# Scores' minimum with a per-row scale in one DVE operation, and squares, sums, masks and first turns moved

## The chip, the cores and the metric

The kernel runs on one core of one Trainium2 chip. The metric is the device time of one execution in microseconds (us). Its engines are named as the profile names them: PE (matrix products), PEld (its weight loads), DVE (vector), ACT (activation), POOL (GpSimd) and SP, whose queue issues every DMA of this kernel. Each engine works through its own list of instructions in order; semaphores tie the lists together.

## What is computed

Two layers on x (2 x 512 x 1024) and a context of 2 x 1024 x 1024. What matters here:

```
x = x + fake_quant(LN(x)) @ fake_quant(ctx)                         # L0 product
x = x + LN(x) @ W.T + b + low-rank experts mixed by a router        # ffn
x = x + attention(LN(x), ctx, ctx, mask)     # 32 query heads, 8 key/value heads, d = 128, rotary
x = x + LN(x) @ W_up.T + low-rank expert of the top gate
softmax:  P = exp(raw/sqrt(d) + mask - rowmax),  out = P V / sum(P),  then out @ wo
```

Products that need more than 16 bits are made of three matmuls, on high and low halves: low by high, high by low, high by high (`mm3`, lines 43 to 45). In attention the halves are float16. Scales that are powers of two, taken from sums of squares of wk, the context, wq and wo, keep the float16 halves in range.

## The kernel before, in words

**Keys and values (to about 435 us).** `steps()` runs 64 steps `s`: a group of four (0 to 3, and 32 to 35 for the second batch), then one at a time. A step multiplies one half of one slice of wv or wk by the transposed context of its batch (24 matmuls), the result ends in one of five PSUM banks, and `kv_end` on DVE, POOL and ACT scales, rotates and splits it before SP stores it. Tables name the step at which side work is done: `SQUARE_STEPS` (squares of wq on ACT, 64 of the 128 tiles; `square`, line 1971, one pass over 128x512 with a sum per row) and `SQUARE_LOAD_STEP` (their loads on SP, seven buffers), `KEY_SUM_AT` (a tiny product on PE that sums squares of one wk slice over the partitions, `key_squares`, line 873, then `key_scale` on DVE), `X_QUANTISE_AT`, `C_QUANTISE_AT`, `SUM_AT` (`sum_product`, line 899, ahead of the step's own products) and `L0_AT` (the L0 product, line 912). At the start ACT splits w0, c0, c1, w1, c2 to c7 into halves (`split_hi`, line 1892) and squares c0 to c7 and w1 (`key_square`, line 1980); on DVE `context_squares` (line 1301) adds the eight sums after splitting w2; PE's `key_squares(0)` needs both. Key sum 5 is at step 20.

**ffn (to about 550 us).** PE turns and multiplies tiles f0 to f7 and turns h0 to h7; ACT takes the roots and high halves, and in between the squares 64 to 127 of wq and wo. SP loads those, stores tiles, and from `load_h` on loads what attention needs.

**Attention (about 550 to 1950 us).** 64 heads H (32 per batch), four row tiles of 128 each, n = 4H + i in all. In every slot (p, w) PE does a quarter of the query product of head p + 2 (`q_part`), a quarter of the output product (`wo_part`), one tile of scores (`scores(4p + w + 3)`, into one of two PSUM pairs) and once per head the values product (`values(p - 1)`). One tile n passes: PE scores; DVE `scores_max` (line 1728: scores + mask written to `psb`, the row maximum accumulated into column i of `c`; then line 1731, a 128x1 multiply by the scale and by -1; its wait on the semaphore of the maximum stands between the two); ACT `exp` (line 2139, scale and bias per row, sum accumulated); DVE `row_scale` (lines 1739 and 1741); ACT `p_hi` (line 2146); DVE `p_lo` (line 1746); SP `turn_p` (line 689, a DMA transpose). ACT's `p_hi(n)` waits for the transpose of n - 3 to land, PE's `scores(n)` for the maximum of n - 2. At the end of a slot group w = 3 DVE rotates the queries (`q_end`), POOL adds and splits them (`q_lo`, lines 2306, 2308), ACT copies the high half (`q_hi`) and then the output's (`o_hi`), DVE its low half (`o_lo`, line 1751), for which `wo_part` waits every second head. POOL also scales and splits the weights of wq and wo that SP streams in (lines 2296, 2302), and SP's loads wait for POOL's earlier splits.

**Entry of attention.** DVE: `q_end(0)`, `scale_mask` of tile 0 (line 1718), `q_end(1)`, mask 1, `scores_max(0)`, `h_lo(7)` (for which PE's `q_part(2, 0)` waits), and so on; `q_end(2)` after slot (0, 0); in slot (0, 1) `output_sums` and `output_scales` (lines 1568 to 1581, twelve operations of at most 16 numbers per row), for which PE has added up the squares of wo and of the value scales (`square_sums("v")`, in slot (0, 1), in bank 7). SP: masks 2 and 3 are issued after `store_h(7)`, which waits for `h_lo(7)`; ahead of `turn_p(1)` stand four weight loads, of which wo (2, 1) waits for POOL's split of wq 6 and wq 9 for that of wq 7.

Of the kernel before, what the change touches and what calls it, by code (L numbers as in the profile page):

```python
# [112 lines left out]
SQUARE_STEPS = sorted([*range(6, 28), *range(38, 60), *range(40, 60)])  # L113
# [8 lines left out]
def build_in(nc, ctx, A, out):  # L122
# [276 lines left out]
    KEY_SUM_AT = {0: 0, 5: 1, 9: 2, 13: 3, 17: 4, 20: 5, 25: 6, 29: 7, 32: "c1"}  # L399
# [48 lines left out]
    v_ws = signal("v_ws", [("w", j) for j in range(11)] + [("v", j) for j in range(12)])  # L448
# [6 lines left out]
    v_nmax = signal("v_nmax", range(256))  # L455
# [99 lines left out]
    def sync_program(e):  # L555
# [163 lines left out]
        for n in range(71, 105):  # L719
            load_square(n)  # L720
        for i in range(4):
            store_h(i)
            for n in (range(105, 110), range(110, 116), range(116, 120), range(120, 125))[i]:
                load_square(n)
# [10 lines left out]
        for n in range(125, 128):  # L735
            load_square(n)
# [21 lines left out]
        load_mask(0, 1)  # L758
        load_w(("q", 6))
        load_v(0)  # L760
# [3 lines left out]
        for i in range(2, 4):  # L764
            load_mask(0, i)
# [4 lines left out]
        for p in range(66):  # L770
# [62 lines left out]
    def tensor_program(e):  # L833
# [89 lines left out]
        def square_sums(what):  # L923
# [6 lines left out]
            else:  # L930
                e.wait_ge(a_sq.sem, a_sq[127])
                e.wait_ge(v_ws.sem, v_ws["v", 1])
                e.wait_ge(v_qr.sem, v_qr[0])
                e.matmul(ps[:, 7, 0:64], twos[:, :], squares[:, 64:128], start=True, stop=True)
                e.matmul(ps[:, 7, 64:80], twos[:, :], sc[:, 32:48], start=True, stop=True).then_inc(t_rt.sem, 1)
# [160 lines left out]
        def scores(n):  # L1096
# [6 lines left out]
            if n < 2:  # L1103
                e.wait_ge(v_x2.sem, v_x2[7 - n, 1])
            else:
# [104 lines left out]
        for w in range(4):  # L1210
            q_part(0, w, 7)
        e.wait_ge(v_rt.sem, v_rt[1, 3])
# [8 lines left out]
        for p in range(66):  # L1221
            for w in range(4):
                if (p, w) == (0, 1):
                    square_sums("v")
# [50 lines left out]
    def vector_program(e):  # L1275
# [272 lines left out]
        def query_scale():  # L1548
# [10 lines left out]
            e.reciprocal(kst[:, 38:40], sc[:, 22:24]).then_inc(v_ws.sem, 1)  # L1559

# [5 lines left out]
        def output_sums():  # L1566
            e.wait_ge(t_rt.sem, t_rt["v"])
            e.tensor_reduce(sc[:, 0:1], ps[:, 7, 0:64], AX, ALU.add).then_inc(v_ws.sem, 1)
            e.tensor_reduce(sc[:, 1:3], ps[:, 7, 64:80].rearrange("p (a b) -> p a b", a=2), AX, ALU.add).then_inc(v_ws.sem, 1)
# [846 lines left out]
```

## Time and profile before

| | |
|---|---|
| three runs | 2071.3, 2071.78 (median), 2072.1 us |
| the profiled execution | 2071.39 us |
| its span, first to last instruction | 2069.6 us |
| mean granted TensorE clock over the span | 0.989 |
| instructions | 26390 |
| scores' maxima (line 1728), exponentials (line 2139) | 256 each |

The profiled execution lies 0.4 us below the median. A row of the timeline gives start and duration in us, then engine, line, operation, written tile <- read tiles, and in brackets how long the engine had been idle and what ended that. PE's records overlap: at full clock one matmul of 512 columns follows another every 0.22 us, though each is written as 0.38.

### The profile page before, as it was taken

The numbers are of one execution on the slowest core, as the hardware profiler recorded it, in microseconds if no ns is written. First come the engines' busy times: TensorE is split into PE (matmuls) and PEld (weight loads), VectorE is DVE, ScalarE is ACT, GpSimd is POOL, SyncE is SP. The second block draws the span as 40 slices with busy tenths as digits, with TensorE's granted clock in tenths as the row PEclk, the third lists the DMA queues.
The fourth block names the chain that finished last, engine by engine and source line by source line (L and its number), as shares of the span: only waits on it lengthen the run. The fifth ranks groups of instructions, "written<-read, shape, count | busy, mean of one in ns | idle before, by whom it ended". The sixth has DMA issues, their size and how long they took to land.

```text
span 2069.6 us, 26390 instructions
## 1 busy us (share of the span) xinstructions
PE 1987.7 (96%) x9136; PEld 1113.4 (54%) x9140; DVE 1639.9 (79%) x2960; ACT 1128.5 (55%) x1722; POOL 1234.6 (60%) x751
## 2 busy tenths in 40 slices
PE   7999999999979999999999999999999999999899
PEld 6877786878634444444444444444444444444487
DVE  5777786576788888888888888888898898888743
ACT  5453553345556666665666665556665666656410
POOL 1542352422158777777777777777777877775500
PEclk9999999999989999999999999999999999999999
DMA  7652575445988787887778798977777787877611
GB/s 247 207 175 89 181 233 165 144 147 189 302 197 166 149 173 146 179 162 157 160 147 174 163 218 198 200 172 163 164 161 158 159 176 147 166 154 149 187 65 69
DMA packets 673382, 349.56 MB, mean 169 GB/s; under 512 B 576769, under 2 KB 601601, under 8 KB 673249
## 3 DMA queue, kind: packets, MB, share of 16 engines
q1 hardware_dynamic: 673248, 347.87, 70.0%
q8 instruction: 73, 1.20, 0.2%
q14 instruction: 61, 0.49, 0.1%
HBM read 173.73 MB, written 31.46 MB: 99 GB/s over the span
## 4 chain that ended last, share of the span: by engine, by line
PE 75%; DVE 8%; issue 3%; DMA 2%; ACT 2%; POOL 1%; SPq 0%; ACTq 0%; DVEq 0%; POOLq 0%
PE ps L43 25%; PE ps L44 24%; PE ps L45 24%; PE ps L912 1%; DMA pT<-pp 1%; POOL u_sb L2253 1%; DVE psb L1728 1%; DVE pp L1746 1%; DVE t_sb L1290 1%; DVE t_sb L1292 1%; DVE u_sb L1289 0%; DVE vhl_sb L1386 0%; PE ps L919 0%; DMA raw<-in_ctx 0%; ACT wh L1892 0%
## 5 line engine op out<-in xcount | busy, mean ns | idle before, releaser
L1746 DVE SCALAR_TENSOR_TENSOR pp<-psb,st,pp 128x1024 f16<-128x1024 f32 x256 | 423.0, 1652 | 3.4 <-ACT pp L2146 1.3
L2139 ACT ACTIVATE psb<-psb,st,sc 128x1024 f32<-128x1024 f32 x256 | 317.6, 1240 | 174.3 <-DVE st L1731 174.3
L2146 ACT ACTIVATE pp<-psb,st 128x1024 f16<-128x1024 f32 x256 | 293.4, 1146 | 165.0 <-DVE st L1741 158.5
L1728 DVE CUSTOM_DVE_ANT_0 psb<-ps,mask 128x1024 f32<-128x1024 f32 x256 | 311.8, 1218 | 32.5 <-PE ps L45 31.2
L2296 POOL TENSOR_SCALAR araw<-araw,kst 128x512 f32<-128x512 f32 x128 | 283.0, 2211 | 49.4 <-DMA araw<-in_wq 49.4
L2296 POOL TENSOR_SCALAR araw<-araw,sc 128x512 f32<-128x512 f32 x128 | 258.3, 2018 | 0.0
L2302 POOL TENSOR_TENSOR wol<-araw,woh 128x512 f16<-128x512 f32 x128 | 149.5, 1168 | 137.5 <-ACT woh L2072 137.5
L43 PE MATMUL ps<-woh,osb 128*128 128x512 f16 x512 | 195.0, 381 | 23.8 <-issue 19.0
L1762 DVE SCALAR_TENSOR_TENSOR x_lo<-ps,sc,x_lo 128x512 f32<-128x512 f32 x256 | 190.4, 744 | 20.4 <-PE ps L45 20.4
L43 PE MATMUL ps<-ksb,qsb 128*128 128x512 f16 x512 | 195.3, 381 | 9.5 <-DVE st L1728 8.1
L43 PE MATMUL ps<-pT,vsb 128*128 128x512 f16 x512 | 194.4, 380 | 6.0 <-DMA pT<-pp 5.2
L44 PE MATMUL ps<-ksb,qsb 128*128 128x512 f16 x512 | 195.3, 381 | 0.0
L45 PE MATMUL ps<-ksb,qsb 128*128 128x512 f16 x512 | 195.1, 381 | 0.0
L44 PE MATMUL ps<-wol,osb 128*128 128x512 f16 x512 | 194.9, 381 | 0.0
L45 PE MATMUL ps<-woh,osb 128*128 128x512 f16 x512 | 194.8, 380 | 0.0
L44 PE MATMUL ps<-pT,vsb 128*128 128x512 f16 x512 | 194.7, 380 | 0.0
L45 PE MATMUL ps<-pT,vsb 128*128 128x512 f16 x512 | 194.6, 380 | 0.0
L43 PE MATMUL ps<-slots,wl 128*128 128x512 f32 x448 | 180.7, 403 | 12.5 <-ACT slots L1892 9.6
L2306 POOL TENSOR_TENSOR ua<-ua,ta 128x512 f32<-128x512 f32 x64 | 137.4, 2146 | 82.9 <-DVE ta L1277 82.9
L2302 POOL TENSOR_TENSOR wql<-araw,wqh 128x512 f16<-128x512 f32 x128 | 149.8, 1171 | 59.5 <-ACT wqh L2072 59.5
L44 PE MATMUL ps<-slots,wh 128*128 128x512 f32 x448 | 177.2, 396 | 0.0
L45 PE MATMUL ps<-slots,wh 128*128 128x512 f32 x448 | 177.0, 395 | 0.0
(303 smaller groups left out, 3946.4 us busy)
## 6 DMA issues: line engine op xcount, KB each, us to landing
araw<-in_wq SPq DMA_DIRECT2D x128, 256.0 KB, 4.5
araw<-in_wo SPq DMA_DIRECT2D x128, 256.0 KB, 4.3
scan<-in_wq SPq DMA_DIRECT2D x64, 256.0 KB, 4.5
scan<-in_wo SPq DMA_DIRECT2D x64, 256.0 KB, 4.9
raw<-in_wv SPq DMA_DIRECT2D x16, 512.0 KB, 4.6
raw<-in_ctxT SPq DMA_DIRECT2D x16, 512.0 KB, 4.0
raw<-in_wk SPq DMA_DIRECT2D x16, 512.0 KB, 5.7
raw<-in_ctx SPq DMA_DIRECT2D x16, 512.0 KB, 4.6
```

Of the source, the lines that this page charges most:

```text
L43: e.matmul(dst, ll, rh, start=start, stop=False)
L44: e.matmul(dst, lh, rl, start=False, stop=False)
L45: return e.matmul(dst, lh, rh, start=False, stop=stop)
L912: m = e.matmul(bank(L0_BANKS[n % 3]), a1T[:, k, i * 128:i * 128 + 128], bq[:, k, nh * 512:nh * 512 + 512], start=k == 0, stop=k == 7)
L1728: e.tensor_tensor_reduce(out=psb[:, n % 3, :], in0=pair(n % 2 * 2), in1=mask[:, i, :], scale=1.0, scalar=LOWEST, op0=ALU.add, op1=ALU.max, ...
L1746: e.scalar_tensor_tensor(out=pp[:, r, 1024:2048], in0=psb[:, r, :], scalar=st[:, n // 4 % 4, 16 + i:17 + i], in1=pp[:, r, 0:1024], op0=ALU ...
L1762: e.scalar_tensor_tensor(out=xs, in0=bank(6 + i % 2), scalar=sc[:, 30 + (q - 2) // 32:31 + (q - 2) // 32], in1=xs, op0=ALU.mult, op1=ALU.a ...
L2139: e.activation(P, P, ACT.Exp, bias=c[:, 4 + i:5 + i], scale=sc[:, 23 - H // 32:24 - H // 32], accum_out=c[:, 8 + i:9 + i]).then_inc(a_exp. ...
L2146: e.activation(pp[:, r, 0:1024], psb[:, r, :], ACT.Copy, scale=st[:, n // 4 % 4, 16 + i:17 + i]).then_inc(a_ph.sem, 1)
L2296: e.tensor_scalar(w_raw(n), w_raw(n), scale, None, ALU.mult).then_inc(p_ws.sem, 1)
L2302: e.tensor_tensor(w_dst(key, 1), w_raw(n), w_dst(key, 0), ALU.subtract).then_inc(p_wlo.sem, 1)
L2306: e.tensor_tensor(ua[:, :], ua[:, :], ta[:, :], ALU.add).then_inc(p_qu.sem, 1)
```

## The change

In `scores_max` the one DVE operation now adds the mask, multiplies by `sc[:, 23 - H//32]`, a value per row that `query_scale` has turned negative with one more small operation, and accumulates the minimum; line 1731 and its semaphore are gone, and `exp` takes the minimum as its bias and -1 as its scale. The rest moves: squares between steps, key sum 5 from step 20 to 21, the start's key squares between the splits, the squares of the ffn stage each a little earlier (none after h5's root), their loads with them; `square_sums("v")` to just after `q_part(0, ...)`, in bank 3, and `output_sums` and `output_scales` to just after `q_end(0)`, ahead of the first mask; `q_end(2)` from slot (0, 0) to (0, 1); on SP masks 2 and 3 ahead of the first values' load and of `store_h(7)`, load wo (2, 1) behind `turn_p(1)` and load wq 9 behind `turn_p(2)`. `SQUARE_STEPS` had one square at steps 6 to 27, 38 and 39 and two at 40 to 59; now one at 8 to 17, 25, 26 and 38, and three at 19, 20, 21, 23, 24 and 48 to 59.

```diff
-SQUARE_STEPS = sorted([*range(6, 28), *range(38, 60), *range(40, 60)])
+SQUARE_STEPS = sorted([*range(8, 18), 38] + [19, 20, 21, 23, 24] * 3 + [25, 26] + [*range(48, 60)] * 3)
-    KEY_SUM_AT = {0: 0, 5: 1, 9: 2, 13: 3, 17: 4, 20: 5, 25: 6, 29: 7, 32: "c1"}
+    KEY_SUM_AT = {0: 0, 5: 1, 9: 2, 13: 3, 17: 4, 21: 5, 25: 6, 29: 7, 32: "c1"}
...
         load_mask(0, 1)
+        load_mask(0, 2)
         load_w(("q", 6))
+        load_mask(0, 3)
         load_v(0)
         store_x2(7)
         store_h(7)
         load_w(("q", 7))
-        for i in range(2, 4):
-            load_mask(0, i)
...
             if p < 64:
                 load_w(("o", p + 2, 0))
+            if 0 < p < 64:
                 load_w(("o", p + 2, 1))
-            if 2 * p + 9 < 128:
-                load_w(("q", 2 * p + 9))
+                if 2 * p + 9 < 128:
+                    load_w(("q", 2 * p + 9))
...
                     turn_p(4 * p + w + 1)
+                if (p, w) == (0, 0):
+                    load_w(("o", 2, 1))
+                if (p, w) == (0, 1):
+                    load_w(("q", 9))
...
             q_part(0, w, 7)
+        square_sums("v")
         e.wait_ge(v_rt.sem, v_rt[1, 3])
...
+            e.wait_ge(v_ws.sem, v_ws["w", 10])
+            e.tensor_scalar(sc[:, 22:24], sc[:, 22:24], -1.0, None, ALU.mult).then_inc(v_ws.sem, 1)
...
-            e.tensor_tensor_reduce(out=psb[:, n % 3, :], in0=pair(n % 2 * 2), in1=mask[:, i, :], scale=1.0, scalar=LOWEST,
-                                   op0=ALU.add, op1=ALU.max, accum_out=c[:, i:i + 1]).then_inc(v_max.sem, 1)
-            e.wait_ge(v_max.sem, v_max[n])
-            e.tensor_scalar(c[:, 4 + i:5 + i], c[:, i:i + 1], sc[:, 23 - H // 32:24 - H // 32], -1.0, ALU.mult,
-                            ALU.mult).then_inc(v_nmax.sem, 1)
+            e.tensor_tensor_reduce(out=psb[:, n % 3, :], in0=pair(n % 2 * 2), in1=mask[:, i, :], scale=sc[:, 23 - H // 32:24 - H // 32],
+                                   scalar=-LOWEST, op0=ALU.add, op1=ALU.min, accum_out=c[:, i:i + 1]).then_inc(v_max.sem, 1)
...
         q_end(0, 7)
+        output_sums()
+        output_scales()
         scale_mask(0, 0)
...
-                if (p, w) == (0, 0):
+                if (p, w) == (0, 1):
                     q_end(2)
-                if (p, w) == (0, 1):
-                    output_sums()
-                    output_scales()
...
         for key in SPLIT_ORDER[:10]:
             split_hi(key)
-            if key in ("c5", "c6", "c7"):
-                key_square(("c", int(key[1:]) - 5))
-        for c in range(3, 8):
-            key_square(("c", c))
+            for done in {"c2": [0], "c3": [1], "c4": [2], "c5": [3, 4], "c6": [5], "c7": [6, 7]}.get(key, []):
+                key_square(("c", done))
         key_square(0)
...
-            e.wait_ge(v_nmax.sem, v_nmax[n])
-            e.activation(P, P, ACT.Exp, bias=c[:, 4 + i:5 + i], scale=sc[:, 23 - H // 32:24 - H // 32], accum_out=c[:, 8 + i:9 + i]).then_inc(a_exp.sem, 1)
+            e.wait_ge(v_max.sem, v_max[n])
+            e.activation(P, P, ACT.Exp, bias=c[:, i:i + 1], scale=-1.0, accum_out=c[:, 8 + i:9 + i]).then_inc(a_exp.sem, 1)
```

## Rows read from the trace of the kernel before

**Rows 1.** The page: busy time, share of the span and instructions of each engine

```profile
PE 1987.7 (96%) x9136; PEld 1113.4 (54%) x9140; DVE 1639.9 (79%) x2960; ACT 1128.5 (55%) x1722; POOL 1234.6 (60%) x751
```

**Rows 2.** Windows: busy us (x instructions) per engine, PEclk, DMA share, GB/s

```profile
36.10:39.50 3.40, 3.40 (x9) 2.61 (x9) 3.07 (x14) 2.57 (x5) 0.00 (x0) 0.50 0.07 22
135.10:141.90 6.80, 5.83 (x15) 4.53 (x16) 4.50 (x10) 3.81 (x9) 2.45 (x2) 0.50 0.54 155
322.90:326.30 3.40, 3.40 (x10) 2.67 (x9) 2.22 (x7) 2.23 (x7) 2.20 (x1) 0.51 1.03 266
589.10:592.50 3.40, 3.25 (x8) 1.16 (x9) 3.19 (x10) 2.14 (x5) 2.38 (x2) 0.51 0.11 22
595.90:602.70 6.80, 6.04 (x15) 2.20 (x16) 5.66 (x13) 5.01 (x7) 0.73 (x1) 0.50 1.10 201
900.00:1100.00 200.00, 196.46 (x904) 87.28 (x903) 171.76 (x302) 123.14 (x170) 153.77 (x94) 1.00 0.78 162
```

**Rows 3.** Waits of PE, whole span: us in total, times, longest us

```profile
PE ps L43 <- DVE st L1728: 8.1, 4, 3.5
...
PE ps L873 <- ACT junk L1980: 3.1, 1, 3.1
...
PE ps L899 <- POOL ctab L2265: 3.0, 1, 3.0
...
PE ps L873 <- DVE ksq L1301: 2.4, 1, 2.4
```

**Rows 4.** Waits of PE from 620 to 1895 us

```profile
PE ps L43 <- issue: 17.3, 24, 1.7
```

**Rows 5.** Timeline (start us, us) around the end of the first step

```profile
30.82 1.06 ACT L1980 ACTIVATE junk<-slots 128x1024 bf16<-128x1024 f32 x1
...
35.40 0.15 DVE L1301 TENSOR_REDUCE ksq<-ksq 128x1 f32<-128x8 f32 x1
```

**Rows 6.** Timeline at step 20 of the key and value stage

```profile
134.78 1.06 ACT L1980 ACTIVATE junk<-wh 128x1024 bf16<-128x1024 f32 x1
```

**Rows 7.** Timeline at steps 47 to 50

```profile
311.63 0.62 ACT L1971 ACTIVATE scan<-scan 128x512 f32<-128x512 f32 x1
...
320.45 2.13 POOL L2265 TENSOR_TENSOR ctab<-ctab,bq 128x1024 f16<-128x1024 f16 x1
```

**Rows 8.** Timeline at the entry of attention

```profile
564.01 1.06 DVE L1718 TENSOR_SCALAR mask<-mask,kst 128x1024 f32<-128x1024 f32 x1 [0.83 <-DMA mask<-in_mask]
...
566.51 0.69 DVE L1277 TENSOR_TENSOR ua<-ps,cosq 128x512 f32<-128x512 f32 x1 [1.44 <-POOL qsb L2308]
...
572.35 0.59 PE L43 MATMUL ps<-hTa,wql 128*128 128x512 f16 x1 [3.12 <-DVE hst L1277]
...
578.35 0.93 DVE L1718 TENSOR_SCALAR mask<-mask,kst 128x1024 f32<-128x1024 f32 x1 [2.23 <-DMA mask<-in_mask]
...
589.36 0.21 DVE L1568 TENSOR_REDUCE sc<-ps 128x1 f32<-128x64 f32 x1
...
589.89 1.12 DVE L1297 TENSOR_SCALAR sc<-sc 128x3 int32<-128x3 int32 x1
...
591.38 3.00 SPq L689 DMA_TRANSPOSE pT<-pp  x1
...
592.75 0.36 DVE L1581 TENSOR_SCALAR vso<-vsc,sc 128x8 f32<-128x8 f32 x2
```

**Rows 9.** Timeline in the middle of attention

```profile
993.43 1.16 POOL L2302 TENSOR_TENSOR wol<-araw,woh 128x512 f16<-128x512 f32 x1 [0.60 <-ACT woh L2072]
993.49 0.21 DVE L1731 TENSOR_SCALAR st<-st,sc 128x1 f32<-128x1 f32 x1
...
993.62 2.05 DVE L1746 SCALAR_TENSOR_TENSOR pp<-psb,st,pp 128x1024 f16<-128x1024 f32 x1
...
995.77 0.15 DVE L1741 TENSOR_SCALAR st<-st 128x1 f32<-128x1 f32 x1
...
1004.54 0.38 PE L43 MATMUL ps<-woh,osb 128*128 128x512 f16 x1 [0.69 <-issue]
```

More of the change, by code:

```diff
@@ L447, in build_in @@
     v_h2 = signal("v_h2", range(8))
-    v_ws = signal("v_ws", [("w", j) for j in range(11)] + [("v", j) for j in range(12)])
+    v_ws = signal("v_ws", [("w", j) for j in range(12)] + [("v", j) for j in range(12)])
     v_rt = signal("v_rt", [(b, j) for b in range(2) for j in range(8)])
@@ L718, in sync_program @@
             load_w(("q", n))
-        for n in range(71, 105):
+        for n in range(71, 113):
             load_square(n)
@@ L722, in sync_program @@
             store_h(i)
-            for n in (range(105, 110), range(110, 116), range(116, 120), range(120, 125))[i]:
+            for n in (range(113, 119), range(119, 124), range(124, 128), [])[i]:
                 load_square(n)
@@ L932, in square_sums @@
                 e.wait_ge(v_ws.sem, v_ws["v", 1])
-                e.wait_ge(v_qr.sem, v_qr[0])
-                e.matmul(ps[:, 7, 0:64], twos[:, :], squares[:, 64:128], start=True, stop=True)
-                e.matmul(ps[:, 7, 64:80], twos[:, :], sc[:, 32:48], start=True, stop=True).then_inc(t_rt.sem, 1)
+                e.wait_ge(v_x2.sem, v_x2[6, 1])
+                e.matmul(ps[:, 3, 0:64], twos[:, :], squares[:, 64:128], start=True, stop=True)
+                e.matmul(ps[:, 3, 64:80], twos[:, :], sc[:, 32:48], start=True, stop=True).then_inc(t_rt.sem, 1)
         def ffn_turn(tile):
@@ L2074, in scalar_program @@
         ffn_hi(4)
-        for n in range(72, 75):
+        for n in range(72, 77):
             square(n)
         root(("f", 6))
-        for n in range(75, 76):
+        for n in range(77, 80):
             square(n)
         ffn_hi(5)
-        for n in range(76, 84):
+        for n in range(80, 89):
             square(n)
@@ L2085, in scalar_program @@
         ffn_hi(6)
-        for n in range(84, 90):
+        for n in range(89, 97):
             square(n)
@@ L2090, in scalar_program @@
         ffn_hi(7)
-        for n in range(90, 98):
+        for n in range(97, 106):
             square(n)
@@ L2096, in scalar_program @@
         router_exp(1)
-        for n in range(98, 101):
+        for n in range(106, 109):
             square(n)
         lora_hi(1)
-        for n in range(101, 103):
+        for n in range(109, 112):
             square(n)
@@ L2103, in scalar_program @@
         h_hi(1)
-        for n in range(103, 109):
+        for n in range(112, 118):
             square(n)
@@ L2107, in scalar_program @@
         h_hi(2)
-        for n in range(109, 113):
+        for n in range(118, 123):
             square(n)
@@ L2111, in scalar_program @@
         h_hi(3)
-        for n in range(113, 118):
+        for n in range(123, 128):
             square(n)
@@ L2115, in scalar_program @@
         h_hi(4)
-        for n in range(118, 121):
-            square(n)
         root(("h", 6))
         h_hi(5)
-        for n in range(121, 125):
-            square(n)
         root(("h", 7))
         h_hi(6)
-        for n in range(125, 128):
-            square(n)
         split_w(("q", 3))
```

11 lines of the change are left out of this document (4 added, 7 removed).

## The prediction

> **What bounds the kernel now.** I read the page first. PE is busy 96% of the span [rows 1], so only what makes PE wait, or run slow, can be gained or lost. The windows then show short stretches in which PE ran at half the granted clock, 1.2 GHz, ten in the span; five stand in [rows 2], each right behind one of PE's waits. PE's waits by releaser name the events: at the start for the key squares' sum (2.4), at step 20 for a key square on ACT (3.1), at step 50 for a sum on POOL (3.0), at the entry of attention for DVE's maxima [rows 3], and in the body of attention 24 waits, 17.3 us together [rows 4]. The timelines around these [rows 5 to 9] say what is late at each. A matmul that is not held follows the last one after 0.22 us whatever DVE does: DVE is busy 171.8 of 200 us in mid-attention, PE 196.5 [rows 2]. DVE time saved is therefore worth nothing by itself; it pays only in front of one of these waits.
>
> **The sum, part by part.** It is made against the profiled execution, 2071.39 us, which lies 0.4 below the median; I forecast the same quantity for the median. A measurement of this kernel tells about 0.2%, 4.1 us, from no change.
>
> *Start.* ACT does six key squares in a row behind c7, 1.24 apart, the last of them at 30.8, then w1's, and only then w2; DVE adds the sums behind w2's low half, at 35.40 [rows 5], and PE waits 2.4. Spread over the gaps between the arriving tiles, the squares end some 3 us sooner, by my replay at 28.5, w2 is split while PE still works on the first group, and the sum is ready at about 32.9, when PE ends it. Gone: 2.4 of wait and half of 3.4 us at half clock, 1.7 [rows 2, 3]; together 4.1. The later splits c3 to c7 come up to 2 us later, but PE reaches c7 only 1.3 or more behind it. DVE's and SP's work moves forward by 2.5 only, so a load of weights may be short: I take 3.4, bounds 1 and 4.1.
>
> *Key sum 5 from step 20 to 21.* PE waits 3.1 for the key square that starts at 134.78 [rows 3, 6], and loses half of 5.8 busy us at half clock, 2.9 [rows 2]. A step later PE has 5.2 us of products in front of the sum. The squares that now crowd steps 19 to 21 stand behind the key square on ACT. What is late next is `a_turn(3)` behind step 22, which needs DVE's `key_scale(5)`; it has a step of time. I take 5.8, bounds 3 and 6.
>
> *Step 50.* PE waits 3.0 for POOL's last sum, 320.45 to 322.6, then loses 1.7 to the clock [rows 2, 3, 7]. That sum hangs on the split of w25 on ACT, which stood behind two squares of 0.62 each [rows 7], and this on an identical pair before w23. All four are gone from the steps 39 to 47: 2.5 off the chain, which leaves 0.5 of wait; I take the low stretch to go with the rest. Of 3.0 + 1.7 that is 4.2 less what rounding of my replay may hide, 4.0; bounds 0 (another wait takes the place) and 4.7. The square dropped at step 27 gives 0.5 at the second batch's start.
>
> *What is added.* Three squares a step from 48 on, and one or two more ahead of the roots of f6 and h2: at each of three places 0.62 or twice that falls on ACT ahead of something PE waits for. The others lie beside ACT's idle time; were that gone, each would cost its 0.62. The small operation behind `query_scale` is one more of 0.2 there. Together 1.5, bounds 0 and 3. DMA bytes are the same; SP's loads of squares come nearer to their use, in steps where ACT has nothing else to do.
>
> *Entry of attention.* Output sums and scales took DVE from 589.36 to 593.1, 3.75 us, of which one operation on three numbers took 1.12 [rows 8]. Now they stand ahead of the first mask, where DVE was idle 0.83 for its DMA and 1.44 for POOL: 2.3 cover, so mask 0, `q_end(1)` and `h_lo(7)` come 1.5 later, and PE's wait of 3.1 at 572.35 [rows 8] grows to 4.6. If nothing blocks the twelve operations (2.0 us) that is 0; if POOL holds each of the last four, 3.7. `square_sums("v")`, 0.6 of PE, moves to where PE stood 0.8 for POOL; it costs nothing. In return, masks 2 and 3 leave the queue that stood behind `h_lo(7)`, and the idle 2.23 before mask 2 [rows 8] goes; the 3.75 leave the chain between the fifth and sixth maximum; and `turn_p(1)`, which left SP's queue at 591.38 [rows 8] although its tile was ready at 582.8, goes out at about 583, so ACT's `p_hi(4)` no longer waits for it. PE spends here 7.4 of the 8.1 us of waits for maxima [rows 3] and half of 3.25 and 6.04 busy us at low clock [rows 2], 12.0 in all. It will not all go: DVE needs 3.0 per tile where PE, with only scores to do, needs 1.3. My replay leaves waits of 1.7, 2.3 and 1.9 before the sixth and seventh scores and the second values product. 12.0 - 1.5 - 5.9 = 4.6; I take 4.2, bounds -2 and 10.
>
> *One operation fewer per tile, 256 times.* From the start of line 1731 to the next start are 0.13 us [rows 9]. The scale as a per-row operand is not in the trace for this operation; line 1731, with one such operand, takes 0.21 and line 1741, with constants alone, 0.15 [rows 9], so I add 0.06 (bounds -0.1 and 1.2, a second pass). Net about 0.1 per tile. But the tile loop does not run on DVE: line 1746 starts at 993.62, POOL's split at 993.43, and 1746 then takes 2.05 where alone it takes 1.28 [rows 9], so it ends 1.07 behind POOL's end. An earlier start waits longer for POOL. Only the last maximum before `q_end` is not behind such a wait. POOL, ACT and `o_lo` then carry that 0.1 to `wo_part`, whose wait (0.69 at 1004.54) is one of the 24. 24 x 0.12 = 2.9, bounds -3 and 17.3.
>
> The Trainium skill (SBUF — State Buffer, Who interferes with whom) has a rule for this: a vector operation with two SBUF inputs, or a two-port one, and a GpSimd one exclude each other, and whoever issues first keeps the shared port to its end. The 2.05 and the 1.12 agree. Without the rule, all three maxima between two syncs would count, 24 x 0.3 = 7.2 in place of 2.9.
>
> *The change of batch and the end.* Exponentials start 0.2 sooner and DVE leads for some four tiles at each: 1.4, bounds 0 and 4.
>
> Sum: 3.4 + 5.8 + 0.5 + 4.0 - 1.5 + 4.2 + 2.9 + 1.4 = 20.7. 2071.4 - 20.7 = 2050.7; I say **2051**, this case's own range 2044 to 2058.
>
> **Rivals.** (A) *The forecast*, 0.57.
>
> (B) *The order on the port turns over.* Line 1746 starts 0.19 behind POOL at 993.43; one operation less is 0.13 of that. Where DVE comes first, it ends 0.8 to 0.9 sooner, `q_end` follows, and all 24 waits vanish: 17.3 in place of 2.9, 2036.5. For it: the margin is 0.06 to 0.1, and eight of 32 head pairs show no such wait even now. Against it: the row operand's 0.06 eats half. 0.15. The skill's rule on the port, by which the first to issue keeps it, is what this would be.
>
> (C) *Early gains are taken back by queues.* The operations ahead of the first mask are each held by POOL (3.7 instead of 1.5, and a second stretch at low clock), so that the entry of attention gives nothing, and at step 50 the context tile's load or the extra DMA is late in place of ACT: 20.7 - 4.2 - 4.0 - 2 = 10.5, 2061. For it: 1.12 and 2.23 [rows 8] show both kinds. 0.20.
>
> (D) *Slower: the minimum with a row scale is not the same pass.* Place: line 1728. DVE has 28 us idle in 200 at mid-attention [rows 2], 0.7 per tile. If the scaled form made two passes, 2.4 instead of 1.2, it would add 1.1 per tile net: (1.1 - 0.7) x 256 = 102, less 17 of the other gains, 2156. It decides from about 1.6 us per operation: each 0.1 above 1.3 costs up to 24 x 0.3 = 7 us at the `wo_part` waits. For: no row shows the form. Against: the add and the maximum already share one pass, and row scales cost 0.06 elsewhere. 0.04.
>
> (E) *Within 0.2%*: (C) with the start's gain lost too to a late weight load and new low-clock stretches. 2068. 0.04.
>
> **Numbers.** Faster: A, B, C, 0.92; same 0.04; slower 0.04. The range 2040 to 2062 leaves out most of B (0.11), D and E: 0.19.
>
> **What would show it.** Right: PE has no wait at the key sums of the first group and step 21, and no half clock there; the sum on POOL at step 50 costs PE under 1 us; line 1728 takes 1.26 to 1.30; line 1731 is gone; the sums and scales stand before the first mask and `h_lo(7)` is 1 to 2 us later relative to `q_end(0)`; `turn_p(1)` goes out within 1 us of its tile; waits of PE for DVE's maxima at the entry fall from 7.4 to about 4; some 24 waits of 0.6 remain before `wo_part`. Wrong: these waits gone (B); a wait over 5 us for `h_lo(7)`, or still 3 at step 50 (C); line 1728 above 1.6 (D); new low-clock stretches between 40 and 130 or 320 and 440.

## The result and the profile after

| | before | changed |
|---|---|---|
| median (runs) | 2071.94 us (4) | 2034.64 us (4) |
| profiled span | 2069.6 us | 2034.3 us |
| ratio, 95% interval | | 0.9819, 0.9802 to 0.9836 |

The change gains 37.3 us, 1.8%. I had forecast 20.7, in a range of 2040 to 2062: the sign was right, the size was not. Run again beside other kernels, the changed kernel gave 0.9835 (0.982 to 0.985); the kernel before had medians of 2069.2 to 2075.6 from one set of runs to the next, so everything below is told as a ratio to its own runs of before, or from one trace. One execution of one variant (`loads_back`) took 4170.5 us, twice the time of its other three, and is in no ratio.

To place the gain I count PE's matmuls. The n-th matmul is the same work in both kernels, so the time between two of them is the length of a stage. Up to four records are missing in a trace (two near 167 us, two near 349), about 1 us. Stages are named by the time they have in the kernel before.

| stage | before | changed, two traces | gained | forecast |
|---|---|---|---|---|
| to 240 us (start, step 20, second batch) | 240.2 | 235.4, 233.7 | 4.8, 6.5 | 9.7 |
| 240 to 540 (step 50, feed-forward) | 299.9 | 299.4, 297.3 | 0.5, 2.6 | 2.5 |
| 540 to 640 (entry of attention) | 100.0 | 92.0, 90.7 | 8.0, 9.3 | 4.2 |
| 640 to 1895 (body of attention) | 1254.9 | 1233.3, 1235.6 | 21.6, 19.3 | 4.3 |
| the rest | 169.8 | 170.4, 169.7 | -0.6, 0.1 | 0 |

The miss is the body. The first line of the page, the windows (columns as in [rows 2]) and PE's waits of the changed kernel:

```profile
PE 1976.0 (97%) x9140; PEld 1114.2 (55%) x9140; DVE 1605.2 (79%) x2705; ACT 1105.9 (54%) x1722; POOL 1247.3 (61%) x751
```

```profile
156.80:160.20 3.40, 3.40 (x9) 1.25 (x10) 3.36 (x4) 3.34 (x12) 0.89 (x1) 0.51 0.24 83
...
566.40:569.80 3.40, 3.40 (x9) 1.14 (x8) 2.89 (x6) 2.82 (x6) 3.26 (x3) 0.51 0.65 207
586.80:590.20 3.40, 3.40 (x11) 1.14 (x9) 3.30 (x9) 2.58 (x5) 0.01 (x1) 0.52 1.03 190
900.00:1100.00 200.00, 199.15 (x921) 89.56 (x920) 167.59 (x267) 122.83 (x174) 159.99 (x97) 1.00 0.80 166
```

Waits of PE in the whole span:

```profile
PE ps L43 <- DVE st L1733: 5.3, 3, 3.1
...
PE ps L914 <- DVE tmp L1437: 4.0, 1, 4.0
...
PE ps L901 <- POOL ctab L2258: 2.2, 1, 2.2
```

and from 620 to 1895 us, against [rows 4]:

```profile
PE ps L43 <- issue: 5.7, 25, 1.4
```

In 200 us of mid-attention PE now does 921 matmuls where it did 904 [rows 2]. The wait ahead of the output product is still there, about as often as before, but it is 0.2 us and no longer 0.7. The half-clock stretches at 36, 135 and 323 us are gone, a new one stands at 156.8 behind a new wait of 4.0 for the first layer's terms, and of the two at the entry that are shown in [rows 2] the long one at 595.9 is gone. Others move from trace to trace: one at 518.7 is in this trace and not in the second one of the changed kernel; the one at the change of batch, at 1299.0 before, is missing here and stands at 1269.6 in the second.

Where in the body PE gets its 21.6 us back can be read from its starts. They follow each other after 0.22, and I add up by how much a start comes later than that, where it is over 0.02:

| us over the pitch, in the body | output product | values product | the rest |
|---|---|---|---|
| before | 21.2 in 24 | 11.8 in 58 | 1.9 |
| changed, two traces | 8.2 in 24, 8.7 in 22 | 4.4 in 5, 5.2 in 7 | 0.7, 1.7 |

So 13.0 come at the output product, 0.54 at each of its 24 late starts, and 7.4 at the values product. Most of the late starts there are of 0.1 to 0.2 us, too short for the list of waits. One of them before, and the same place in the changed kernel, in the timeline of PE:

```profile
995.49 0.38 PE L45 MATMUL ps<-ksb,qsb 128*128 128x512 f16 x1
995.92 0.38 PE L43 MATMUL ps<-pT,vsb 128*128 128x512 f16 x1
```

```profile
977.65 0.38 PE L45 MATMUL ps<-ksb,qsb 128*128 128x512 f16 x1
977.86 0.38 PE L43 MATMUL ps<-pT,vsb 128*128 128x512 f16 x1
```

The first pair is 0.43 apart, the second 0.21.

### The profile page after: what moved, and what is told of

Same layout as the page of the kernel before. It is cut to its first block, busy times and chain, and to the rows that moved or that the text cites. A ratio compares the mean times of both kernels' runs of the same rounds, so it can differ in the third digit from the quotient of the medians.

```text
span 2034.3 us, 26140 instructions
## 1 busy us (share of the span) xinstructions
PE 1976.0 (97%) x9140; PEld 1114.2 (55%) x9140; DVE 1605.2 (79%) x2705; ACT 1105.9 (54%) x1722; POOL 1247.3 (61%) x751
## 4 chain that ended last, share of the span: by engine, by line
PE 78%; DVE 7%; issue 2%; DMA 2%; ACT 1%; POOL 1%; SPq 1%; ACTq 0%; DVEq 0%; POOLq 0%
PE ps L43 25%; PE ps L44 25%; PE ps L45 25%; PE ps L914 1%; DMA pT<-pp 1%; POOL u_sb L2246 1%; DVE pp L1748 1%; DVE psb L1733 1%; DVE t_sb L1293 1%; DVE t_sb L1295 1%; PE ps L921 0%; SPq L688 0%; DVE vhl_sb L1389 0%; DVE u_sb L1292 0%; PE ps L1175 0%
## 5 line engine op out<-in xcount | busy, mean ns | idle before, releaser
L1748 DVE SCALAR_TENSOR_TENSOR pp<-psb,st,pp 128x1024 f16<-128x1024 f32 x256 | 403.8, 1577 | 2.6 <-ACT pp L2139 0.5
L2132 ACT ACTIVATE psb<-psb,st 128x1024 f32<-128x1024 f32 x256 | 294.1, 1149 | 174.1 <-DVE st L1733 173.9
L1733 DVE CUSTOM_DVE_ANT_0 psb<-ps,mask,sc 128x1024 f32<-128x1024 f32 x256 | 328.0, 1281 | 71.4 <-PE ps L45 71.2
L2289 POOL TENSOR_SCALAR araw<-araw,kst 128x512 f32<-128x512 f32 x128 | 316.3, 2471 | 46.6 <-DMA araw<-in_wq 46.6
L2289 POOL TENSOR_SCALAR araw<-araw,sc 128x512 f32<-128x512 f32 x128 | 243.4, 1902 | 0.5 <-DMA araw<-in_wo 0.5
L2299 POOL TENSOR_TENSOR ua<-ua,ta 128x512 f32<-128x512 f32 x64 | 127.4, 1991 | 73.4 <-DVE ta L1280 73.4
```

The lines of the kernel that those rows point to most:

```text
L1733: e.tensor_tensor_reduce(out=psb[:, n % 3, :], in0=pair(n % 2 * 2), in1=mask[:, i, :], scale=sc[:, 23 - H // 32:24 - H // 32], scalar=-LOW ...
L1748: e.scalar_tensor_tensor(out=pp[:, r, 1024:2048], in0=psb[:, r, :], scalar=st[:, n // 4 % 4, 16 + i:17 + i], in1=pp[:, r, 0:1024], op0=ALU ...
L2132: e.activation(P, P, ACT.Exp, bias=c[:, i:i + 1], scale=-1.0, accum_out=c[:, 8 + i:9 + i]).then_inc(a_exp.sem, 1)
L2289: e.tensor_scalar(w_raw(n), w_raw(n), scale, None, ALU.mult).then_inc(p_ws.sem, 1)
L2299: e.tensor_tensor(ua[:, :], ua[:, :], ta[:, :], ALU.add).then_inc(p_qu.sem, 1)
```

## The experiments

The changed kernel itself ran once more as a reference:

> The changed kernel as it is, a reference beside the others of this call. Every theory: 0.981 to 0.983 of the kernel before.

Measured: 0.9835 (0.982 to 0.985).

The code cuts below are shortened: names and arguments that do not change are left out.

### The operation per tile, alone and undone

`min_alone` is the kernel before with the minimum in one operation and nothing else, `max_back` the changed kernel with both old operations.

```diff
-  tensor_tensor_reduce(scale=1.0, scalar=LOWEST, ADD, MAX, accum_out=c[i])     # max_back has these back
-  wait v_max[n]; tensor_scalar(c[4 + i], c[i], sc, -1.0, MULT, MULT)
+  tensor_tensor_reduce(scale=sc, scalar=-LOWEST, ADD, MIN, accum_out=c[i])     # min_alone has this
```

> The kernel before with the one operation per tile alone (the minimum of scaled, negated scores; the exponential with a constant scale). The whole change gained 37 us, and from the first tiles of attention to the last, PE came 20 us nearer to its start. Theory (gain adds up tile by tile): the operation saves a little on DVE and 0.09 us on ACT at every one of 256 tiles, and each head pair starts earlier by what the last one gained: 20 us here, 2052, with the waits before the output products down from 24 of 0.6 us to about 0.2 each. Rival (my forecast: the gain is absorbed at each wait for POOL and counts once per wait): 3 to 4 us, 2068. Rival (the body needs the other moves, as the order of loads, too): 8 to 12 us, 2061.

Measured: 0.991 (0.989 to 0.993), 18.7 us by the ratio, 20 by the medians; the body takes 1234.0.

> The changed kernel with the maximum and its negation back as two operations and the exponential's scale as a row operand; all moves stay. If the tile operation carries 20 us by itself: 2035 + 20 = 2055. If the moves carry part of it: 2043 to 2048. By my forecast's step for it (4 us): 2039.

Measured: 0.9926 (0.9905 to 0.9947), 2055.2; body 1251.5. One is the other's mirror: the tile operation gives about 20 us by itself and all the moves together 15 to 17. In `min_alone` PE's lateness in the body is 7.3 at the output product and 6.0 at the values product, as in the changed kernel. No move is needed for it, and it doesn't help the moves.

### What of it counts: DVE's time or the chain to the exponential

`op_kept` issues the small operation again, with its own wait for the minimum, but lets nobody wait for it. `exp_scale` takes the exponential's scale from a column that holds -1.

```diff
+  wait v_max[n]; tensor_scalar(c[4 + i], c[i], sc, -1.0, MULT, MULT)   # op_kept: result unused
...
-  activation(P, P, Exp, bias=c[i], scale=-1.0, accum_out=c[8 + i])     # exp_scale
+  activation(P, P, Exp, bias=c[i], scale=sc[:, 24:25], accum_out=c[8 + i])
```

> The changed kernel, and after each minimum the small operation of before is still issued on DVE (its result is not used; the exponential does not wait for it). It gives DVE back its time, not the wait in the chain. If DVE's time is what counts, the 20 us come back: about 2052. If the chain from scores to exponential counts, or ACT's shorter exponential: 2036 to 2041.

Measured: 0.9943 (0.9922 to 0.9964), 22 to 26 us over the changed kernel's two ratios; body 1257.1, more than before; PE's lateness is 22.6 at the output product and 13.9 at the values product. DVE's time is what counts; the exponential here waits for nothing new. That it is more than before fits the price of the operation, which is 0.25 here and 0.20 in the step from the kernel before (see below).

> The changed kernel, with the exponential's scale (-1) read from a row operand in place of a constant: ACT's exponential should take 1.24 us again in place of 1.15, and nothing else changes. If ACT's 0.09 per tile is a full part of the chain of a head pair (0.09 x 256 = 23 us at most): 2045 to 2055. If ACT has slack and DVE alone counts: 2035 to 2037.

Measured: 0.9845 (0.9824 to 0.9867); body 1237.1, 1.5 to 3.8 over the changed kernel. The exponential takes 1.24 us again instead of 1.15. The constant scale is worth 2 to 5 us by the ratios, a term that I had left out; the intervals don't separate it from nothing.

### The operation at one tile of four

Here is DVE in one head of the kernel before, from the timeline (start, duration, in brackets the idle time before and who ended it):

```profile
967.39 1.23 DVE L1728 CUSTOM_DVE_ANT_0 psb<-ps,mask 128x1024 f32<-128x1024 f32 x1 [0.54 <-PE ps L45]
968.54 0.08 DVE L1728 DVE_READ_ACCUMULATOR2_ANT st<- 128x1 f32 x1
968.66 0.21 DVE L1731 TENSOR_SCALAR st<-st,sc 128x1 f32<-128x1 f32 x1
968.79 1.67 DVE L1746 SCALAR_TENSOR_TENSOR pp<-psb,st,pp 128x1024 f16<-128x1024 f32 x1
...
971.30 1.21 DVE L1728 CUSTOM_DVE_ANT_0 psb<-ps,mask 128x1024 f32<-128x1024 f32 x1
...
972.69 2.05 DVE L1746 SCALAR_TENSOR_TENSOR pp<-psb,st,pp 128x1024 f16<-128x1024 f32 x1
...
975.57 1.22 DVE L1728 CUSTOM_DVE_ANT_0 psb<-ps,mask 128x1024 f32<-128x1024 f32 x1
...
976.96 0.68 DVE L1277 TENSOR_TENSOR ua<-ps,cosq 128x512 f32<-128x512 f32 x1
...
982.76 0.75 DVE L1751 SCALAR_TENSOR_TENSOR osb<-ps,vso,osb 128x512 f16<-128x512 f32 x1 [2.13 <-ACT osb L2154]
983.42 1.22 DVE L1728 CUSTOM_DVE_ANT_0 psb<-ps,mask 128x1024 f32<-128x1024 f32 x1
```

and the same head in the changed kernel:

```profile
949.58 1.28 DVE L1733 CUSTOM_DVE_ANT_0 psb<-ps,mask,sc 128x1024 f32<-128x1024 f32 x1 [0.55 <-PE ps L45]
950.78 0.08 DVE L1733 DVE_READ_ACCUMULATOR2_ANT st<- 128x1 f32 x1
950.78 1.28 DVE L1748 SCALAR_TENSOR_TENSOR pp<-psb,st,pp 128x1024 f16<-128x1024 f32 x1
...
953.46 1.28 DVE L1733 CUSTOM_DVE_ANT_0 psb<-ps,mask,sc 128x1024 f32<-128x1024 f32 x1 [0.28 <-PE ps L45]
...
954.67 1.87 DVE L1748 SCALAR_TENSOR_TENSOR pp<-psb,st,pp 128x1024 f16<-128x1024 f32 x1
...
957.37 1.28 DVE L1733 CUSTOM_DVE_ANT_0 psb<-ps,mask,sc 128x1024 f32<-128x1024 f32 x1
...
958.57 0.69 DVE L1280 TENSOR_TENSOR ua<-ps,cosq 128x512 f32<-128x512 f32 x1
...
964.37 0.75 DVE L1753 SCALAR_TENSOR_TENSOR osb<-ps,vso,osb 128x512 f16<-128x512 f32 x1 [2.13 <-ACT osb L2147]
```

Three things are to be seen.

First, from one maximum to what follows it are 1.40 us before (967.39 to 968.79) and 1.20 after: 0.20 is gone per tile, not 0.1. The row scale does cost the 0.06 of my forecast: the record is 1.28 in place of 1.22, and the read-out of the accumulator starts 1.20 to 1.21 behind the operation's start in all 256 tiles, where it was 1.14 to 1.15. But what follows now starts together with the read-out, while the small operation, whose wait for the maximum stands ahead of it, started 0.12 behind the read-out and then took its 0.13: 0.12 + 0.13 - 0.06 = 0.19. Put back into the changed kernel the operation costs the whole 0.25.

Second, before, DVE waits for PE at 967.39 and then not once for as long as 0.15 us until the output product at 1004.54 [rows 9]: one unbroken run of DVE through two heads, with seven maxima in it. The 2.13 ahead of `o_lo` is no slack either; it is the way round over POOL (rotation's sum) and two casts on ACT, the same 2.13 in both kernels. After, the last wait for PE ahead of the output product at 985.98 is at 974.18.

Third, the subtraction behind the first tile's maximum took 1.67 and takes 1.28; over the heads of the body its mean falls from 1.71 to 1.36. The timeline of POOL beside it, before:

```profile
968.70 1.57 POOL L2296 TENSOR_SCALAR araw<-araw,kst 128x512 f32<-128x512 f32 x1
```

and after:

```profile
950.88 2.61 POOL L2289 TENSOR_SCALAR araw<-araw,kst 128x512 f32<-128x512 f32 x1
```

POOL was 0.09 ahead of DVE's 968.79; now it starts 0.10 behind DVE's 950.78, and it is POOL that takes longer, 2.61 in place of 1.57. That is the order on the port of my rival B, turned over, at another place than I had named. It is also the rule of the Trainium skill (SBUF — State Buffer, Who interferes with whom) that whoever issues first keeps the port for its whole instruction and the other is fully blocked. In who is held, this pair of lines agrees. In how long it does not: with the port kept to POOL's end at 970.27, a subtraction that takes 1.28 alone could not have ended at 970.46. Where the subtraction starts behind this scaling in the trace of before, it ends 0.20 behind POOL's end (39 of 42 places); behind POOL's split, which has two inputs, it ends 1.08 behind (134 of 136). From the two, my estimate is that the scaling lets go some 0.9 before its record ends, though records of POOL are rough.

So the operation was put back behind a single tile's minimum of each head, 64 times, result unused, with `if i == k` around it; the tiles come in the order 3, 0, 1, 2, and then the rotation.

> The changed kernel, with the small operation back (result unused) behind one minimum in four, the first tile's of each head: it stands right before the DVE subtraction that in the kernel before started 0.09 us behind POOL's scaling and took 1.67 us, and in the changed one starts 0.10 ahead of it and takes 1.28. Theory (the order on the port): 0.13 later puts DVE behind POOL again, 64 x (0.13 + 0.39) = 33 us of DVE, of which waits for PE absorb a part; I expect 2047 to 2055 and the 1.67 us subtractions back. Rival (DVE's time alone): 64 x 0.13 = 8 us at most, 2037 to 2043.

> The same number of small operations, 64, behind the third tile's minimum of each head, the last before the rotation, where no POOL operation starts near. Theory (order on the port): only 0.13 each, 8 us at most, 2037 to 2043, and clearly less than with the operation at the first tile. Rival (DVE's time alone): the same time as with the operation at the first tile, within 2 us.

> The changed kernel with the small operation back (result unused) behind the fourth tile's minimum of each head, the one right behind the output's low half. In the changed kernel four waits of DVE for PE follow it in the same head (0.32, 0.31, 0.55, 0.28 us) before the rotation. Theory (an operation costs only what no later wait for PE takes up): nearly free, 0 to 3 us over the changed kernel. Rival (DVE's time counts wherever it is spent): 8 to 14 us, as at the first and third tile.

> The same behind the second tile's minimum, which in the changed kernel starts right at DVE's last wait for PE (0.28) before the rotation, the next minimum following without a wait. Theory: each of the 64 costs its full 0.2 to 0.25 on the chain to the output product, 12 to 15 us over the changed kernel, as at the third tile (14). Rival (only the last one before the rotation counts): 0 to 5 us.

Seven traces have the changed kernel's code in the body (the two of itself and those of `squares_spread`, `squares_39`, `start_back`, `sums_late` and `loads_back`); it takes 1231.6 to 1236.2 in them, so 1 or 2 us in the last column are nothing.

| kept behind tile | waits of DVE for PE between it and the rotation, per head | ratio | body, over 1233.3 |
|---|---|---|---|
| 3 | 4 | 0.9845 (0.9830 to 0.9860) | 1.1 |
| 0 | 1 (0.28) | 0.9848 (0.9830 to 0.9867) | 8.1 |
| 1 | none | 0.9840 (0.9822 to 0.9857) | 1.5 |
| 2 | none | 0.9872 (0.9854 to 0.9891) | 14.2 |
| all four | | 0.9943 (0.9922 to 0.9964) | 23.8 |

The port alone does not explain it: I expected tile 0 to be the dearest, and tile 2 costs more. The number of waits for PE alone does not either: I expected tile 1 to cost 12 to 15, and it costs nothing that can be told. Why is in the timeline of the kernel with the operation behind tile 1:

```profile
957.76 0.21 DVE L1738 TENSOR_SCALAR st<-st,sc 128x1 f32<-128x1 f32 x1
957.89 1.62 DVE L1753 SCALAR_TENSOR_TENSOR pp<-psb,st,pp 128x1024 f16<-128x1024 f32 x1
```

The subtraction starts 0.25 later behind its maximum and takes 1.62 instead of 1.87, so it ends where it ended: POOL, 0.6 ahead of it, holds it to the same moment. Behind tile 2 there is neither a POOL operation that holds DVE nor a wait for PE, as the timeline of that kernel shows:

```profile
959.66 1.27 DVE L1734 CUSTOM_DVE_ANT_0 psb<-ps,mask,sc 128x1024 f32<-128x1024 f32 x1
...
960.98 0.21 DVE L1738 TENSOR_SCALAR st<-st,sc 128x1 f32<-128x1 f32 x1
961.11 0.68 DVE L1281 TENSOR_TENSOR ua<-ps,cosq 128x512 f32<-128x512 f32 x1
```

1.45 from the maximum to the rotation in place of 1.20, and 14.2 / 64 = 0.22 of it arrive at PE. Tile 3 has the waits for PE behind it, tile 0 one of 0.28 and a subtraction that loses the port again (1.61 in that trace in place of 1.28); the waits take up most of that. The four single prices, 1.1 + 8.1 + 1.5 + 14.2 = 24.9, add up to the price of all four, 23.8, as near as bodies can be told apart. They arrive at different places: of tile 2's, 13.3 is lateness at the output product (21.5 in 26) and under 1 at the values product (5.3), of tile 0's 5.1 is at the one (13.3 in 22) and 3.2 at the other (7.6 in 34). The ratios show the same order only for tile 2 and for all four. For tile 0 the ratio says 3 to 6 us over the changed kernel's two, with intervals that overlap; in its own set of runs its median is 7.6 us over that of `squares_spread`, whose body is the changed kernel's, and tile 2's is 12.1 over it.

### Work moved from ahead of the rotation to behind it

If the run through the rotation to the output product is what PE waits for, more can be taken off it.

```diff
     wo_add(p, w)                                   # add_late: not for w == 3
+    if w == 3: q_end(p + 2, ...)                   # rotation_first
     scores_max(n + 3)
...
-  q_end(p + 2, ...)                                # rotation_first
   q_end(p + 2, ...)
+  wo_add(p, 3)                                     # add_late
```

> The changed kernel with the query rotation of each head issued on DVE ahead of the third tile's minimum instead of behind it; its product is done on PE some 3 us before that. Theory (the chain through the rotation sets the wait before the output product): the rotation and all behind it come 1.2 us earlier in each head, PE's remaining 0.3 per two heads goes, and with it up to 10 us at the batch change and in the body: 2026 to 2033. Rival (the minimum, now 2.1 later, becomes what PE waits for): 2038 to 2060, with waits of PE for DVE's minima in the body.

> The changed kernel with the last addition of each head's output product moved on DVE from ahead of the third tile's minimum to behind the rotation, 0.66 off the same chain. Theory: the 0.3 per two heads goes, 5 to 8 us: 2028 to 2032. Rival (the bank that the addition frees is late, 2.7 us, and PE waits for it): 2040 or more, with waits of PE for the addition in each head.

Measured: 0.9769 (0.9753 to 0.9784) and 0.9775 (0.9759 to 0.9791): both beat the changed kernel, by 9 to 14 us with its 0.9819 or 0.9835. The body takes 1225.5 and 1224.8. PE's waits from 620 to 1860 us in the first:

```profile
PE ps L43 <- DMA pT<-pp: 3.6, 4, 1.7
...
PE ps L43 <- issue: 0.6, 2, 0.3
```

The wait ahead of the output product is gone from all but one place, near 1856 us (the other of the two is ahead of a values product), though the third tile's minimum now comes 2.1 later and nobody waits for it in this stretch. It stands in the idle time ahead of `o_lo`, of which 0.80 of the 2.13 are left: the time was on the way of the chain, but it had room for work that is not.

### The stages ahead of attention

`squares_spread` and `sum21_alone`:

```diff
-SQUARE_STEPS = sorted([*range(8, 18), 38] + [19, 20, 21, 23, 24] * 3 + [25, 26] + [*range(48, 60)] * 3)
+SQUARE_STEPS = sorted([*range(6, 28), *range(9, 14), 38] + [*range(48, 60)] * 3)       # squares_spread
...
-    KEY_SUM_AT = {... 17: 4, 20: 5, ...}                                               # sum21_alone, on before
+    KEY_SUM_AT = {... 17: 4, 21: 5, ...}
```

How the new wait of 4.0 comes about stands in the timeline of the changed kernel, ACT and DVE:

```profile
141.02 0.19 ACT L1972 ACTIVATION_READ_ACCUMULATOR scan<-scan 128x1 f32 x1
141.11 1.03 ACT L1893 CAST wh<-raw 128x1024 fp32r<-128x1024 f32 x1
142.05 1.25 ACT L1907 ACTIVATE vhl_sb<-ps,vsc 128x512 f16<-128x512 f32 x2
142.83 1.41 DVE L1389 SCALAR_TENSOR_TENSOR vhl_sb<-ps,vsc,vhl_sb 128x512 f16<-128x512 f32 x2 [4.25 <-ACT vhl_sb L1907]
...
154.49 1.33 DVE L1418 TENSOR_SCALAR small<-small,scal 128x4 f32<-128x4 f32 x1
155.92 0.75 DVE L1437 SCALAR_TENSOR_TENSOR tmp<-ps,small,ctab 128x512 f32<-128x512 f32 x1
```

Six squares end at 141.0 on ACT, then a split, then the value pieces; DVE stands 4.25 for these, everything behind them on DVE is late, and the first term that PE waits for at 152 us comes at 155.92, the operation before it (1.33 for 128x4) being held by a sum on POOL as well.

> The changed kernel with the first squares spread again over steps 6 to 27 (one a step, two in five early ones) instead of three a step at 19 to 21, 23 and 24; steps 48 on as changed. In the changed kernel ACT does six squares and a split ahead of the value pieces at step 21, DVE waits 4.25 us for these, and PE then 4.0 for the first layer's terms at 152 us, with a half-clock stretch of 3.4 behind it. Theory (the crowd on ACT): that wait and the low clock go, 4 to 5.7 us: 2030. Rival (with the wait at step 20 gone PE is simply early, and the next wait takes its place whatever ACT does): 2034 to 2036, the wait at 152 stays.

Measured: 0.9813 (0.9798 to 0.9828), no change. The wait shrinks to 2.2 and its low clock goes, 3 us earlier at 190 us; at the second batch's start PE then waits 3.2 with a low stretch behind, and at 240 us 1.1 are left, or nothing against the second trace of the changed kernel. Both theories hold a part: the crowd made 1.8 of the 4.0 (1.2 of the 3.4 in the second trace), and a lead of PE is spent at the next thing that is late.

> The kernel before with the sixth key sum at step 21 in place of 20, alone; the squares stay where they were. Theory (crowd): PE gains the 3.1 of wait and 2.9 of clock and keeps them: 2066. Rival (PE simply early): the gain shows at 140 us and is taken back before 165: 2070 to 2072.

Measured: 0.9982 (0.9971 to 0.9992). At 140 us PE is 6.3 ahead (1.3 of it from the start), at 190 only 3.8 with a wait of 2.2 for the same term, though no squares crowd here, and at 640 it is behind. The trace goes the rival's way, the time only in part: the ratio is a gain of 1.7 to 6 us, so it is not shown that nothing is left.

`squares_alone` puts the new steps on the kernel before, `squares_39` gives the changed one `[*range(38, 60), *range(45, 60)]` in place of `38` and `[*range(48, 60)] * 3`; `start_back` has the eight key squares back in their old order, six of them behind the last split.

> The kernel before with the new steps of the first 64 squares, alone. My forecast's step: at step 50 the wait of 3.0 for POOL and its low clock shrink to 0.5 and none, 4 us, less 1.5 for the squares added later, and with key sum 5 still at step 20 the squares crowded there make that wait longer or leave it: 2068 to 2072. Rival (the wait at step 50 hangs on the rotation through DVE and POOL and not on the split behind the squares): it stays at 2.5 to 3.3, and the time is 2071 to 2075.

Measured: 0.9979 (0.9965 to 0.9993). The wait at step 50 in its timeline:

```profile
321.24 0.60 PE L899 MATMUL ps<-ctab,onesb 128*128 128x512 f16 x2 [1.02 <-POOL ctab L2265]
```

1.0 instead of 3.0, with no half clock behind it: 2.0 + 1.7 = 3.7 of my 4.0. At step 20 the crowd makes the wait 4.6 instead of 3.1, as expected.

> The changed kernel with squares again from step 38 on, one a step and two from 45 on, in place of three a step from 48. Theory: at step 50 the wait for POOL's last sum is 3.0 again and its low clock returns (2.5 of loss), while from 400 to 530 us the 2.3 that the crowd cost there come back: 2034 to 2037. Rival (the crowd from 48 on costs nothing, its losses are others'): 2037 to 2038. Rival (the split that feeds the sum was late for another reason): the wait at 315 us stays at 2.2 and the time at 2033.

Measured: 0.984 (0.9827 to 0.9854). At step 50 the wait stays (a pitch of 2.7 in place of 2.6) and no low clock returns, and the stage to 540 us is as in the changed kernel. One square a step up to step 44 costs nothing that shows. It is no full undo, as before there were two a step from 40 on, so it says nothing against `squares_alone`; the crowd from 48 on shows no price either.

> The changed kernel with the key squares at the start in their order of before, eight of them behind the last split. Theory: PE's wait of 2.4 at 33 us and 3.4 us of half clock come back, 4.1 in all, and stay: 2038 to 2039. Rival (being early at the start is taken back by 65 us, where 0.9 of it went already, or later at step 24): 2036 to 2037.

Measured: 0.9851 (0.9829 to 0.9873). PE is 6.2 us behind at 40 us and 0.8 at 240, or 2.5 against the second trace of the changed kernel. The wait of 3.6 and 6.8 us of half clock come back, and the wait of 4.0 shrinks to 1.4 with no low clock. The trace shows the rival: most of the start's gain is spent at 152 us. The ratio lies 3 to 7 us over the changed kernel's two, with intervals that overlap, and decides nothing.

### The entry of attention

`sums_late` puts `output_sums`, `output_scales` and `square_sums("v")` back to the second tile, with their banks and waits; `loads_back` gives SP its old order.

> The changed kernel with the output sums and scales (and the product of squares that feeds them) back inside attention's second tile, behind the third rotation. The entry of attention gained 8.5 us in the changed kernel where I had forecast 4.2. Theory (the 3.75 us of DVE that stood between the fifth and sixth maximum were the third of PE's waits): that wait of about 3 and its stretch at low clock return, less what the first one shrinks: 2039 to 2041, with the wait for the first tile's low half near 2 in place of 3.4. Rival (the loads and turns on the queue are what counts): within 1 us of the changed kernel.

Measured: 0.984 (0.9819 to 0.9860). In the trace, PE is 3.7 us further behind at 590 us, with one wait for a maximum of 5.8 in place of 3.1, and no less wait for `h_lo(7)` (3.3). The place of the sums is worth 3 to 4 us in the trace; the ratio can't tell it from nothing.

> The changed kernel with the queue of loads at the entry of attention in its order of before: masks 2 and 3 behind the weights, two more weights ahead of the second turn. If the queue held the entry, 2 to 5 us come back, 2037 to 2040, and the second turn goes out 5 us or more behind its tile; if DVE alone did, 2035 to 2036. Body of attention: the same as in the changed kernel.

Measured: 0.9865 (0.9847 to 0.9883), 6 to 10 us over the changed kernel. In the trace PE loses 2.5 by 590 us and 4.5 between there and 700, where a turned tile comes 3.1 late with half clock behind; the body is 1231.6, unchanged. The order of the loads is worth at least as much as the place of the sums.

## Why the prediction was right and wrong

**Where it failed: one operation fewer per tile.** The step said "the tile loop does not run on DVE ... An earlier start waits longer for POOL. Only the last maximum before `q_end` is not behind such a wait", and priced it 24 x 0.12 = 2.9, with 1.4 more for the change of batch. The body gained 19 to 22. The path was wrong and each factor too small. (a) The saving per tile is 0.20, read off the starts of before (1.40) and after (1.20). The 0.06 for the row operand was right; what I had not seen is the 0.12 by which the small operation started behind the read-out. Nor was my working even: 0.13 less 0.06 is 0.07, and I counted 0.12. (b) I let each of the 24 waits gather the saving of one maximum. DVE runs through two heads without a wait for PE, and each of the 24 fell by 0.54, 13.0 in all; the last maximum before the rotation, kept in all 64 heads, carries 14 us. (c) The values product, for which the same tile loop delivers, was in no term: 58 of its starts were late, and 7.4 came back there. (d) "Waits longer for POOL" is shown for one tile of four, tile 1, which costs nothing that can be told; behind tile 3 stand four waits for PE besides. At tile 0 POOL did not hold its place: its split waits for a cast on ACT, that stands behind a copy which waits for DVE, so POOL moves with DVE, and here DVE passed it. Undoing that at tile 0 costs 8. I had taken one place, 993.43, for the pattern of all. My own figure for "no rule", 7.2, was short too.

**Slack on DVE.** In (D) I took DVE's idle 28 us in 200 for slack. Most of it is the 2.13 per head ahead of `o_lo`, which is on the way of the chain. `op_kept` shows how little slack there was: 0.25 per tile gives all of the gain back.

**Start.** The wait of 2.4 and the half clock went, 4.1 us at 40 us as the step's full term, but what stands at 240 us is 0.8 to 2.5. I had priced the term against its own wait and not against the next one.

**Key sum 5.** The wait of 3.1 and its clock went (5.0 at 140 us), and a wait of 4.0 with a low stretch came at step 24. The step named `a_turn(3)` as late next; that wasn't late, the first layer's terms were. "The squares that now crowd steps 19 to 21 stand behind the key square on ACT" was true and missed that they stand ahead of the value pieces. Start, sum and batch boundary gave 4.8 to 6.5 of 9.7.

**Step 50.** Right in size when it stands alone (3.7 of 4.0); which of the four squares held the split is not shown, as `squares_39` puts one a step back and leaves the wait. In the changed kernel the wait is 2.2 and 1.6 in the two traces, I take it because PE arrives earlier; the low clock is gone. The price of the added squares, 1.5, can't be told from the stage's total of 0.5 to 2.6 against 2.5.

**Entry.** 8.0 to 9.3 against 4.2, inside the bounds of -2 to 10. The waits for maxima are 4.5 as forecast (about 4), and the third wait and the long half-clock stretch are gone. `h_lo(7)` came later by 0.25 and not by 1.5, although two of the small operations ahead of the first mask were held (1.00 and 1.13 us), and PE's waits of 0.8 and 1.4 for POOL before it went too, 2.2 that were in no term. The order of SP's queue had more in it than the one turned tile that I counted.

**The rivals.** (B) comes near in time (2036.5 against 2034.6), and that is in part luck. The order on the port did turn over, but at another subtraction than line 1746 at 993.62, which is held as before (1.87 to 2.05), and undoing it costs 8 us of the 20; 14 hang on a maximum with no POOL operation behind it. Nor did the 24 waits vanish: they fell from 17.3 to 5.7, and what (B) counted too much there was made up at the values product and the entry. (C) was right that early gains are taken back, but at 152 us, behind ACT's work, and not at the entry; (D) did not occur, line 1733 shows 1.28. With the chance of (B) at 0.15 the range ended above it.

## What to carry to other kernels

Ask of an engine in a loop where its last wait for the bound engine lies before the result that the bound engine waits for. What is saved behind that wait pays on every turn of the loop (tile 2 here, 14 us), unless a third engine holds the helper to a fixed moment on the way (tile 1, nothing that can be told). What is saved ahead of it pays little (tile 3), unless it turns an order on a port (tile 0, 8 us). An idle time that repeats to a hundredth (2.13 here) can be a way round through other engines: it is no slack for the chain that runs through it, but it has room for other work. Look also at starts that are late by less than the list of waits shows: 58 of them gave back 7 us here. The same look finds the next change, as moving the rotation one operation forward did for 0.5 to 0.7% more. A gain early in a pipeline is worth what is left of it at the next thing that is late: look 100 us further on before counting it.

## What the runs showed of the hardware that I had not expected

The reducing operation of 128x1024 with a per-row scale is 0.06 us longer than with a constant: its record is 1.28 and not 1.22, and its accumulator is read out 1.20 behind its start and not 1.14. An independent operation starts together with that read-out; a small one that waits for the maximum starts 0.12 later, so it costs 0.25 of DVE in all, about twice its pitch of 0.13. On ACT the scale as a constant makes the 128x1024 exponential 1.15 us, as a row operand 1.24. And a tenth of a microsecond in the order of DVE's subtraction and POOL's scaling decides which of them is stretched: 1.67 and 1.57, or 1.28 and 2.61. And how long POOL holds DVE depends on POOL's operation: the subtraction ends 0.20 behind the end of POOL's scaling and 1.08 behind that of its two-input split.
